# A conditioned attention and state-space block: transposes of u put together ahead of C's, and softplus's guard moved from VectorE to ScalarE

## The chip, the cores and the metric

The kernel runs on one core of one Trainium2 chip. TensorE (PE, with its weight loads listed apart as PEld), VectorE (DVE), ScalarE (ACT), GpSimd (POOL) and SyncE (SP, which only issues transfers here) run side by side, each working down its own list of instructions in order, and wait for each other by semaphores. The metric is the device time of one execution in microseconds (us); lower is better.

## The reference, cut to what matters

The inputs are 8 batch items of 1024 rows by 512 columns. An attention block comes first, then a selective state-space layer. The change touches only the part of that layer between its convolution and its recurrence:

```python
u = silu(conv(x_in))                              # 1024 steps x 1024 channels
x_dbl = u @ x_proj_w.T                            # 64 + 16 + 16 columns
dt_r, B, C = split(x_dbl, [64, 80])
dt = softplus(dt_r @ dt_proj_w.T + dt_proj_b)
def step(h, (dt_t, B_t, C_t, u_t)):               # 16 states per channel
    h = h * exp(dt_t[:, :, None] * A) + (dt_t * u_t)[:, :, None] * B_t[:, None, :]
    y = einsum('bdn,bn->bd', h, C_t)
y = ys + u * D_param                              # then gated by silu(z) and projected
```

## The kernel before

The batch items are worked one after the other (loop `b`). Within an item the attention comes first, then the projections, then the convolution; while an item's recurrence runs, PE and ACT fill their gaps with the previous item's output products and with the next item's front part.

Channels lie on the partitions in 8 tiles of 128 (index n, `ND = NT = 8`), time along the free dimension (1024). The recurrence works on 4 tiles at a time (`DL = 4`), in two groups (`DG = 2`). For each of the 16 states (round r) and each of the 4 tiles, ACT computes the decay exp(dt*A) into PSUM (L892), POOL computes dt*u*B (L693, `inject`), DVE runs the scan (L1172, printed by the order as a SCALAR_TENSOR_TENSOR that writes area_h), PE transposes the state back to rows of time (L1509), and DVE (L1182, `add`) and ACT (L876, `scale_by_c`) each take half of the product with C.

Ahead of the first group's scans stands a stretch that this change rearranges. PE ends the products for x_dbl, and ACT copies them to `xdT` (L870). PE then transposes u, 8 blocks for each of 8 row tiles (L1433, into the PSUM bank pairs 4-5 and 6-7 in turn; tile n may start once DVE has emptied tile n-2), and DVE multiplies each by D into the accumulator (L1147; below "the products with D", signal `s_ai`). Among these PE transposes C (L1439, into banks 2-3) and DVE copies it to `C_nat` (L1151, signal `s_cn`). PE projects dt for one channel tile at a time (`project_dt`, two matrix products of 512 columns through L1251, signal `s_dp`) into the bank pairs 0, 2, 6, 4 for the tiles n mod 4 = 0, 1, 2, 3.

Softplus of a tile takes these steps: DVE adds the bias and takes the minimum with 30 (`clip`, L1139, signal `s_dm`); ACT takes the exponential (L882) and log(1 + x) (L884, signal `s_dl`), both in `soft`; DVE takes the maximum of the result and the unclipped value (L1160, signal `s_dt`) and multiplies u by dt (L1163, signal `s_du`), both in `dt_and_dtu`. Tiles 0 to 3 pass through before the first group's scans and among them, tiles 4 to 7 at the turn from the first group to the second. ACT's list there is: soft(4), one `scale_by_c`, soft(5), one `scale_by_c`, the decay of tile 4, two `scale_by_c`, the decay of tile 5, soft(6), the decay of tile 6, soft(7), the decay of tile 7. The order on every engine is written out by hand; no scheduler moves anything.

Of the kernel before, what the change touches and what calls it, by code (L numbers as in the profile page):

```python
# [9 lines left out]
ACT = mybir.ActivationFunctionType  # L10
P = 128
# [131 lines left out]

    return slice(i, i + n) if isinstance(i, int) else bass.ds(i, n)

PRO = 10


COLS = {}
# [20 lines left out]
def build(nc, x, condT, mask, params, q_w, k_w, v_w, v_b, emb_w, emb_b, out_w, out_b,  # L170
          adaT, ada_b, inT, xpT, dtT, D_row, opT, out):
    ctx = ExitStack()
    with ctx:
        def sb(name, shape):
            return ctx.enter_context(nc.sbuf_tensor(name, shape, F32))
# [89 lines left out]
        def col(name, i, n=1):  # L265
            at = COLS[name][0]
            return par[:, at + i:at + i + n]
# [8 lines left out]
        den = sb("den", [P, TILES])  # L276
        rden = sb("rden", [P, TILES])
        warm = sb("warm", [P, 1])
        z_st = sb("z_st", [P, 512])
        vb_row, ones_row = wdt[96:P, 0:D], wdt[96:P, D:D + P]  # L280

# [13 lines left out]
        def banks(i, n=TB):  # L295
            return ps[:, i:i + n, :].rearrange("p a c -> p (a c)")
# [445 lines left out]
        def _(act):  # L742
# [64 lines left out]
            for b in range(B):  # L807
# [70 lines left out]

                def soft(n):

                    act.wait_ge(*s_dm.at(b, n + 1))
                    nc.scalar.activation(dtmp[:, n % DL, :], dtmp[:, n % DL, :], ACT.Exp).then_inc(s_de.sem, 1)  # L882
                    act.wait_ge(*s_de.at(b, n + 1))
                    nc.scalar.activation(dtmp[:, n % DL, :], dtmp[:, n % DL, :], ACT.Ln, bias=1.0).then_inc(s_dl.sem, 1)  # L884

# [92 lines left out]
        def _(dve):  # L978
# [25 lines left out]
                at += 4  # L1004
            dve.wait_ge(s_ea.sem, 1)
            v.tensor_scalar_mul(negA[:, :], negA[:, :], -1.0).then_inc(s_pro.sem, 1)
            assert at + 1 == PRO
            dve.wait_ge(s_pro.sem, PRO)

            def row_stats(N, src, n):  # L1010
# [35 lines left out]
            for b in range(B):  # L1046
# [87 lines left out]
                                               scalar=col("cw", n * DC + i), in1=cv[:, n % 2, :],  # L1134
                                               op0=ALU.mult, op1=ALU.add).then_inc(s_cv.sem, 1)

                def clip(n):
                    dve.wait_ge(*s_dp.at(b, n + 1))
                    v.tensor_scalar(dtmp[:, n % DL, :], banks(DT_BANK[n % DL]), col("dtb", n), 30.0,  # L1139
                                    ALU.add, ALU.min).then_inc(s_dm.sem, 1)  # L1140


                dve.wait_ge(*s_xpd.at(b, 32))
                dve.wait_ge(*s_x1s.at(b, 16))
                for n in range(NT):
                    dve.wait_ge(*s_ut.at(b, n + 1))
                    v.tensor_tensor(acc[n], ps[:, 4 + 2 * (n % 2):6 + 2 * (n % 2), :], D_bc.rearrange("p (h c) -> p h c", h=DG),  # L1147
                                    ALU.mult).then_inc(s_ai.sem, 1)
                    if n == 1:
                        dve.wait_ge(*s_ct.at(b, 1))  # L1150
                        v.tensor_copy(C_nat[:, :, :], banks(2).rearrange("p (n c) -> p n c", n=NT)[:, :, DTR + NS:XD]  # L1151
                                      ).then_inc(s_cn.sem, 1)
                        clip(0)
                    if n == 3:
                        clip(1)
                dve.wait_ge(*s_ai.at(b, NT))
                dve.wait_ge(*s_cn.at(b, 1))
                def dt_and_dtu(n):
                    dve.wait_ge(*s_dl.at(b, n + 1))
                    v.scalar_tensor_tensor(out=dT[:, n % DL, :], in0=banks(DT_BANK[n % DL]), scalar=col("dtb", n),  # L1160
# [22 lines left out]
                                           op0=ALU.mult, op1=ALU.add).then_inc(s_acc.sem, 1)  # L1183

                dt_and_dtu(0)
                clip(2)
                dt_and_dtu(1)
                clip(3)
                scan(0, 0, 0, 0)
                dt_and_dtu(2)  # L1190
                scan(0, 0, 0, 1)
# [8 lines left out]
                for dl in range(DL):  # L1200
                    scan(0, NS - 1, 1, dl)
                    add(0, NS - 2, 2 * dl)
                clip(4)
                clip(5)
                add(0, NS - 1, 0)
                add(0, NS - 1, 2)
                dt_and_dtu(4)
                add(0, NS - 1, 4)
                dt_and_dtu(5)
                add(0, NS - 1, 6)  # L1210
                clip(6)
                scan(1, 0, 0, 0)
                dt_and_dtu(6)
                clip(7)
                scan(1, 0, 0, 1)
                dt_and_dtu(7)
                scan(1, 0, 0, 2)
# [29 lines left out]
        def _(pe):  # L1247
# [79 lines left out]
            for b in range(B):  # L1327
# [95 lines left out]
                def project_dt(n):  # L1423
                    for th in range(TB):
                        done = mm(ps[:, DT_BANK[n % DL] + th, :], wdt[0:DTR, n * P:(n + 1) * P],
                                  xdT[0:DTR, th * 512:(th + 1) * 512], 0, 0)
                    done.then_inc(s_dp.sem, 1)

                for n in range(NT):
                    if n >= 2:  # L1430
                        pe.wait_ge(*s_ai.at(b, n - 1))
                    for k in range(ND):
                        last = nc.tensor.transpose(ps[:, 4 + 2 * (n % 2) + k // 4, (k % 4) * P:(k % 4 + 1) * P],  # L1433
                                                   U[:, k, n * P:(n + 1) * P], ident[:, :])
                    last.then_inc(s_ut.sem, 1)
                    if n == 1:
                        pe.wait_ge(*s_xde.at(b, 1))
                        for m in range(NT):
                            last = nc.tensor.transpose(ps[:, 2 + m // 4, (m % 4) * P:(m % 4 + 1) * P],  # L1439
                                                       xdT[:, m * P:(m + 1) * P], ident[:, :])  # L1440
                        last.then_inc(s_ct.sem, 1)
                        project_dt(0)
                    if n == 2:
                        pe.wait_ge(*s_cn.at(b, 1))
                        project_dt(1)
                pe.wait_ge(*s_ai.at(b, NT))
                def start_unit(i):
                    if emptied_first(i):
# [41 lines left out]
                            deferred_product(m)  # L1490

                project_dt(2)
                project_dt(3)
                for dg in range(DG):
                    pe.wait_ge(*s_dt.at(b, (dg + 1) * DL))
# [99 lines left out]
```

## Time and profile before

| | |
|---|---|
| median of 3 runs | 6619.38 us (6618.05 to 6626.11) |
| the profiled execution | 6618.08 us, of which its span is 6616.3 us |
| PE busy | 6091.8 us (92%) |
| DVE busy | 5758.6 us (87%) |
| ACT busy | 4575.9 us (69%) |
| POOL busy | 3036.3 us (46%) |
| mean granted TensorE clock | 0.949 of full speed |

Busy shares are means over stages with different limits. In the timeline a row gives the start from the beginning of the span, the time that the merged instructions took, their engine, line, operation, output and inputs; in brackets stands the idle time of the engine just before, with the instruction that ended it. A row with x8 stands for 8 instructions of a kind in a run. On DVE and ACT an instruction's row overlaps the next one's by some tenths of a microsecond, so that the distance between starts is shorter than the duration shown. PE's products in 32-bit floating point appear as two instructions each.

### The profile page before, as it was taken

The page shows a single profiled execution, that of the slowest core. Times are in us where ns is not written, and L with a number is a line of the kernel's source. Part 1 is how long each engine was busy: PE and PEld are TensorE (multiplying, and loading weights), DVE is VectorE, ACT ScalarE, POOL GpSimd, SP SyncE. Part 2 cuts the span into 40 slices and gives each one's busy share as a digit, 9 for nine tenths or more (in the row PEclk, how much of TensorE's full clock was granted, in tenths as well). Part 3 has the DMA queues.
Part 4 walks back from the last instruction along what each step waited for, and adds up shares of the span by engine and source line. Part 5 has one row for each costly group of instructions (what it writes and reads, how often), then busy time and mean ns, then how long its engine had stood idle before and what let it go on. Part 6 is the DMA issues. An engine that isn't in the chain of part 4 may idle for free.

```text
span 6616.3 us, 114602 instructions
## 1 busy us (share of the span) xinstructions
PE 6091.8 (92%) x43104; PEld 3972.8 (60%) x43104; DVE 5758.6 (87%) x7083; ACT 4575.9 (69%) x6560; POOL 3036.3 (46%) x1538
## 2 busy tenths in 40 slices
PE   5998999988999889989899899998899988999877
PEld 2774558645585556845577455774558655685554
DVE  0797999889997999969999799988999789996995
ACT  2775678667786677857778467866778667785653
POOL 0104881068701786019830388105871078601883
PEclk8999999999999999999999999999999999999967
DMA  3535885357834678247863488535784467824764
GB/s 144 172 96 163 204 204 156 115 166 199 237 106 143 166 204 233 85 143 185 216 190 101 146 207 207 160 109 165 195 219 129 136 165 199 240 72 146 178 147 129
DMA packets 326517, 1087.52 MB, mean 164 GB/s; under 512 B 49944, under 2 KB 50072, under 8 KB 286960
## 3 DMA queue, kind: packets, MB, share of 16 engines
q1 hardware_dynamic: 245728, 656.81, 31.0%
q0 software_dynamic: 61840, 390.09, 26.2%
q10 hardware_dynamic: 18432, 33.56, 1.5%
q8 instruction: 344, 5.64, 0.4%
q14 instruction: 173, 1.42, 0.1%
HBM read 570.16 MB, written 241.71 MB: 123 GB/s over the span
## 4 chain that ended last, share of the span: by engine, by line
PE 68%; DVE 21%; issue 5%; POOL 2%; DMA 2%; ACT 2%; SPq 1%; DVEq 0%; ACTq 0%; POOLq 0%
PE ps L1251 39%; DVE area_h L1172 13%; PE ps L1359 13%; PE ps L1509 8%; DVE area_acc L1182 4%; PE ps L1300 3%; POOL area_s L693 2%; PE ps L1302 1%; PE ps L1272 1%; DVE area_dt L1160 1%; DVE area_h L1139 1%; PE ps L1433 1%; PE ps L1456 1%; DVE area_acc L1147 1%; DMA k_stack<-qk_keep 1%
## 5 line engine op out<-in xcount | busy, mean ns | idle before, releaser
L693 POOL TENSOR_TENSOR area_s<-area_u,area_s 128x1024 f32<-128x1024 f32 x1024 | 2495.1, 2450 | 602.2 <-DVE area_u L1163 370.0
L1172 DVE TENSOR_TENSOR_SCAN area_h<-ps,area_s 128x1024 f32<-128x1024 f32 x1024 | 2332.7, 2278 | 18.4 <-POOL area_s L693 17.1
L1509 PEld LDWEIGHTS ps<-ident,area_h 128*128 128x128 f32 x8192 | 984.5, 150 | 776.7 <-DVE area_acc L1182 431.8
L1509 PE MATMUL ps<-ident,area_h 128*128 128x128 f32 x8192 | 1192.0, 293 | 207.2 <-DVE area_acc L1182 142.3
L814 ACT ACTIVATE area_s<-area_s,negmax 128x1024 f32<-128x1024 f32 x1024 | 1179.0, 1151 | 251.4 <-DVE negmax L1068 242.8
L1068 DVE CUSTOM_DVE_ANT_0 area_s<-ps,area_dt 128x1024 f32<-128x1024 f32 x1024 | 1242.8, 1215 | 102.6 <-PE ps L1251 102.1
L892 ACT ACTIVATE ps<-area_dt,negA 128x1024 f32<-128x1024 f32 x1024 | 1146.2, 1119 | 241.3 <-DVE area_h L1172 100.8
L681 POOL TENSOR_TENSOR area_s<-area_s 128x1024 f32<-128x1024 f32 x64 | 161.5, 2524 | 2302.3 <-ACT area_s L867 2302.3
L876 ACT ACTIVATE area_w<-ps,C_nat 128x512 f32<-128x512 f32 x1024 | 703.6, 687 | 688.0 <-PE ps L1509 680.5
L1359 PE MATMUL ps<-ident,area_s 128*128 128x128 f32 x8192 | 1062.0, 272 | 0.4
L1359 PEld LDWEIGHTS ps<-ident,area_s 128*128 128x128 f32 x8192 | 955.1, 141 | 139.2 <-issue 5.2
L1251 PE MATMUL ps<-area_xT,area_w 128*128 128x512 f32 x2048 | 932.3, 594 | 10.7 <-ACT k_stack L791 7.8
L1182 DVE SCALAR_TENSOR_TENSOR area_acc<-ps,C_nat,area_acc 128x512 f32<-128x512 f32 x1024 | 744.0, 727 | 60.8 <-PE ps L1509 60.5
L1087 DVE COPY area_h<-ps 128x512 f32<-128x512 f32 x1024 | 705.4, 689 | 69.1 <-PE ps L1359 63.8
L1251 PE MATMUL ps<-k_stack,q_stack 128*128 128x512 f32 x2048 | 734.7, 440 | 18.6 <-DVE negmax L1068 14.2
L1251 PE MATMUL ps<-area_w,area_xT 128*128 128x512 f32 x1536 | 713.8, 599 | 0.5 <-ACT area_xT L759 0.4
L1251 PEld LDWEIGHTS ps<-area_xT,area_w 128*128 128x128 f32 x2048 | 375.1, 190 | 396.4 <-issue 351.9
L823 ACT ACTIVATE area_h<-ps 128x512 f32<-128x512 f32 x1024 | 589.9, 577 | 10.1 <-PE ps L1359 10.0
L1251 PE MATMUL ps<-area_h,area_u 128*32 128x128 f32 x16384 | 552.5, 276 | 8.6 <-ACT area_h L823 7.0
L1251 PEld LDWEIGHTS ps<-area_h,area_u 128*32 128x32 f32 x16384 | 417.2, 109 | 94.7 <-issue 88.0
L1133 DVE SCALAR_TENSOR_TENSOR area_h<-area_h,par 128x1024 f32<-128x1024 f32 x192 | 290.8, 1523 | 189.9 <-ACT area_h L859 185.3
L1251 PEld LDWEIGHTS ps<-area_w,area_xT 128*128 128x128 f32 x1536 | 274.2, 193 | 248.5 <-issue 248.5
(124 smaller groups left out, 5294.8 us busy)
## 6 DMA issues: line engine op xcount, KB each, us to landing
area_acc<-area_w POOLq DMA_DIRECT2D x256, 1024.0 KB, 7.6
area_s<-b_rows SPq DMA_DIRECT2D x256, 512.0 KB, 4.3
q_stack<-qk_keep SPq DMA_DIRECT2D x512, 128.0 KB, 2.8
k_stack<-qk_keep SPq DMA_DIRECT2D x512, 128.0 KB, 3.1
area_s<-z_keep SPq DMA_DIRECT2D x72, 512.0 KB, 5.0
qk_keep<-q_stack SPq DMA_DIRECT2D x128, 256.0 KB, 4.6
qk_keep<-k_stack SPq DMA_DIRECT2D x128, 256.0 KB, 4.8
y_keep<-area_acc POOLq DMA_DIRECT2D x8, 4096.0 KB, 14.8
```

The lines of the kernel that those rows point to most:

```text
L693: pool.tensor_tensor(dbu[:, dl % 2, :], U[:, k // (NS * DL) * DL + dl, :], bb[:, q, :], ALU.mult).then_inc(s_dbu.sem, 1)
L814: nc.scalar.activation(S[:, t % SR, :], S[:, t % SR, :], ACT.Exp, scale=-1.0, bias=negmax[:, t % TILES:t % TILES + 1], accum_out=den[:, t ...
L823: nc.scalar.activation(PT[:, (t // HALF) % 2, HALF:NT, c * P:(c + 1) * P], ps[:, ring_bank("act", t), :].rearrange("p (m c) -> p m c", m=H ...
L876: nc.scalar.activation(part[slot][:, n // 2, :], ps[:, 5, :], ACT.Identity, scale=C_nat[:, n, r:r + 1]).then_inc(s_ev.sem, 1)
L892: nc.scalar.activation(banks(2 * (dl % 2)), dT[:, dl, :], ACT.Exp, scale=negA[:, a_col:a_col + 1]).then_inc(s_da.sem, 1)
L1068: v.tensor_tensor_reduce(out=S[:, t % SR, :], in0=banks(2 * (t % 2)), in1=mask_add, scale=-1.0, scalar=3.0e38, op0=ALU.add, op1=ALU.min, a ...
L1087: v.tensor_copy(PT[:, (t // HALF) % 2, 0:HALF, c * P:(c + 1) * P], ps[:, ring_bank("dve", t), :].rearrange("p (m c) -> p m c", m=HALF)).th ...
L1172: v.tensor_tensor_scan(out=hs[:, q, dl, :], data0=banks(2 * (dl % 2)), data1=dbu[:, dl % 2, :], initial=0.0, op0=ALU.mult, op1=ALU.add).th ...
L1182: v.scalar_tensor_tensor(out=part, in0=ps[:, 4, :], scalar=c_col, in1=part, op0=ALU.mult, op1=ALU.add).then_inc(s_acc.sem, 1)
L1251: return nc.tensor.matmul(out, lhsT, rhs, start=(k == 0), stop=(k == last))
L1359: last = nc.tensor.transpose(ps[:, ring_bank(who, t), m * P:(m + 1) * P], S[:, t % SR, (c * HALF + m) * P:(c * HALF + m + 1) * P], ident[: ...
L1509: last = nc.tensor.transpose(ps[:, 4 + n % 2, dl * P:(dl + 1) * P], hs[:, r % 2, dl, n * P:(n + 1) * P], ident[:, :])
```

## The change

1. DVE's `clip` is gone, in all eight places. In `soft`, ACT now reads the projection from PSUM and computes relu(16 - bias - x) with scale -1 and a bias column `below_cap`, then exp(16 - that), with scale -1 and a bias column `cap`. This is exp(min(x + bias, 16)). The logarithm is as before. The two columns are made once, ahead of the batch loop, by two small DVE instructions.
2. On PE the transposes of C come after all of u's, into banks 4-5; the projection of dt for tile 1 comes after u's fifth tile instead of the third. The wait for C's copy stands ahead of the projection of tile 3.
3. On DVE the copy of C comes behind the first `dt_and_dtu` instead of behind the second product with D.

```diff
-PRO = 10
+PRO = 12
+CAP = 16.0
...
                 def soft(n):
+                    act.wait_ge(*s_dp.at(b, n + 1))
+                    nc.scalar.activation(dtmp[:, n % DL, :], banks(DT_BANK[n % DL]), ACT.Relu, scale=-1.0,
+                                         bias=below_cap[:, n:n + 1]).then_inc(s_dm.sem, 1)
                     act.wait_ge(*s_dm.at(b, n + 1))
-                    nc.scalar.activation(dtmp[:, n % DL, :], dtmp[:, n % DL, :], ACT.Exp).then_inc(s_de.sem, 1)
+                    nc.scalar.activation(dtmp[:, n % DL, :], dtmp[:, n % DL, :], ACT.Exp, scale=-1.0, bias=cap[:, 0:1]
+                                         ).then_inc(s_de.sem, 1)
...
+            v.tensor_scalar(below_cap[:, :], col("dtb", 0, ND), -1.0, CAP, ALU.mult, ALU.add).then_inc(s_pro.sem, 1)
+            v.memset(cap[:, :], CAP).then_inc(s_pro.sem, 1)
...
-                def clip(n):
-                    dve.wait_ge(*s_dp.at(b, n + 1))
-                    v.tensor_scalar(dtmp[:, n % DL, :], banks(DT_BANK[n % DL]), col("dtb", n), 30.0,
-                                    ALU.add, ALU.min).then_inc(s_dm.sem, 1)
...
-                    if n == 1:
-                        dve.wait_ge(*s_ct.at(b, 1))
-                        v.tensor_copy(C_nat[:, :, :], banks(2).rearrange("p (n c) -> p n c", n=NT)[:, :, DTR + NS:XD]
-                                      ).then_inc(s_cn.sem, 1)
-                        clip(0)
-                    if n == 3:
-                        clip(1)
...
                 dt_and_dtu(0)
-                clip(2)
+                dve.wait_ge(*s_ct.at(b, 1))
+                v.tensor_copy(C_nat[:, :, :], banks(4).rearrange("p (n c) -> p n c", n=NT)[:, :, DTR + NS:XD]
+                              ).then_inc(s_cn.sem, 1)
                 dt_and_dtu(1)
-                clip(3)
+                dve.wait_ge(*s_cn.at(b, 1))
                 scan(0, 0, 0, 0)
...
-                clip(4)
-                clip(5)
                 add(0, NS - 1, 0)
...
-                clip(6)
                 scan(1, 0, 0, 0)
                 dt_and_dtu(6)
-                clip(7)
...
                     if n == 1:
                         pe.wait_ge(*s_xde.at(b, 1))
-                        for m in range(NT):
-                            last = nc.tensor.transpose(ps[:, 2 + m // 4, (m % 4) * P:(m % 4 + 1) * P],
-                                                       xdT[:, m * P:(m + 1) * P], ident[:, :])
-                        last.then_inc(s_ct.sem, 1)
                         project_dt(0)
-                    if n == 2:
-                        pe.wait_ge(*s_cn.at(b, 1))
+                    if n == 4:
                         project_dt(1)
+                pe.wait_ge(*s_ai.at(b, NT - 1))
+                for m in range(NT):
+                    last = nc.tensor.transpose(ps[:, 4 + m // 4, (m % 4) * P:(m % 4 + 1) * P],
+                                               xdT[:, m * P:(m + 1) * P], ident[:, :])
+                last.then_inc(s_ct.sem, 1)
                 pe.wait_ge(*s_ai.at(b, NT))
...
                 project_dt(2)
+                pe.wait_ge(*s_cn.at(b, 1))
                 project_dt(3)
```

On PE, between the products for x_dbl and the first group's state transposes, the kernel before has these rows (`ident,area_u` are u's transposes, `ident,xdT` C's, `xdT,wdt` the projections of dt):

```order
L1433 MATMUL ps<-ident,area_u 128x128 x16
L1439 MATMUL ps<-ident,xdT 128x128 x8
L1251 MATMUL ps<-xdT,wdt 128x512 x2
L1433 MATMUL ps<-ident,area_u 128x128 x8
L1251 MATMUL ps<-xdT,wdt 128x512 x2
L1433 MATMUL ps<-ident,area_u 128x128 x40
L1251 MATMUL ps<-xdT,wdt 128x512 x4
```

In the changed kernel the same place on PE reads:

```order
L1425 MATMUL ps<-ident,area_u 128x128 x16
L1243 MATMUL ps<-xdT,wdt 128x512 x2
L1425 MATMUL ps<-ident,area_u 128x128 x24
L1243 MATMUL ps<-xdT,wdt 128x512 x2
L1425 MATMUL ps<-ident,area_u 128x128 x24
L1435 MATMUL ps<-ident,xdT 128x128 x8
L1243 MATMUL ps<-xdT,wdt 128x512 x4
```

C's transposes moved from third to next to last, and tile 1's projection two of u's tiles later; the sum of the work is the same.

On ACT, at the turn from the first group of channels to the second, the kernel before has (`area_h<-area_h` are softplus's exponential and logarithm, `ps<-area_dt,negA` a decay, `area_w<-ps,C_nat` a product with C):

```order
L882 ACTIVATE area_h<-area_h 128x1024
L884 ACTIVATE area_h<-area_h 128x1024
L876 ACTIVATE area_w<-ps,C_nat 128x512
L882 ACTIVATE area_h<-area_h 128x1024
L884 ACTIVATE area_h<-area_h 128x1024
L876 ACTIVATE area_w<-ps,C_nat 128x512
L892 ACTIVATE ps<-area_dt,negA 128x1024
L876 ACTIVATE area_w<-ps,C_nat 128x512 x2
L892 ACTIVATE ps<-area_dt,negA 128x1024
L882 ACTIVATE area_h<-area_h 128x1024
L884 ACTIVATE area_h<-area_h 128x1024
```

The changed kernel has there:

```order
L884 ACTIVATE area_h<-ps,below_cap 128x1024
L887 ACTIVATE area_h<-area_h,cap 128x1024
L890 ACTIVATE area_h<-area_h 128x1024
L878 ACTIVATE area_w<-ps,C_nat 128x512
L884 ACTIVATE area_h<-ps,below_cap 128x1024
L887 ACTIVATE area_h<-area_h,cap 128x1024
L890 ACTIVATE area_h<-area_h 128x1024
L878 ACTIVATE area_w<-ps,C_nat 128x512
L898 ACTIVATE ps<-area_dt,negA 128x1024
L878 ACTIVATE area_w<-ps,C_nat 128x512 x2
L898 ACTIVATE ps<-area_dt,negA 128x1024
L884 ACTIVATE area_h<-ps,below_cap 128x1024
```

Each softplus has one instruction more, and no table load (ACT_TABLE_LOAD) has been added between them.

## Rows read from the trace of the kernel before

**Rows 1.** The page: busy time, and the chain that ended last by engine.
```profile
PE 6091.8 (92%) x43104; PEld 3972.8 (60%) x43104; DVE 5758.6 (87%) x7083; ACT 4575.9 (69%) x6560; POOL 3036.3 (46%) x1538
PE 68%; DVE 21%; issue 5%; POOL 2%; DMA 2%; ACT 2%; SPq 1%; DVEq 0%; ACTq 0%; POOLq 0%
```

**Rows 2.** Timeline of DVE (start, us, engine, line, ...), second item, first group.
```profile
1366.69 2.36 DVE L1147 TENSOR_TENSOR area_acc<-ps,area_h 128x1024 f32<-128x1024 f32 x2 [8.62 <-PE ps L1433]
1368.96 0.28 DVE L1151 COPY C_nat<-ps 128x128 f32<-128x128 f32 x1
1370.25 1.28 DVE L1139 TENSOR_SCALAR area_h<-ps,par 128x1024 f32<-128x1024 f32 x1 [1.01 <-PE ps L1251]
...
1374.21 1.22 DVE L1147 TENSOR_TENSOR area_acc<-ps,area_h 128x1024 f32<-128x1024 f32 x1 [1.54 <-PE ps L1433]
...
1382.45 1.28 DVE L1160 SCALAR_TENSOR_TENSOR area_dt<-ps,par,area_h 128x1024 f32<-128x1024 f32 x1
...
1384.91 1.28 DVE L1139 TENSOR_SCALAR area_h<-ps,par 128x1024 f32<-128x1024 f32 x1
...
1389.78 2.27 DVE L1172 TENSOR_TENSOR_SCAN area_h<-ps,area_s 128x1024 f32<-128x1024 f32 x1
...
1401.64 4.63 DVE L1172 TENSOR_TENSOR_SCAN area_h<-ps,area_s 128x1024 f32<-128x1024 f32 x2 [0.32 <-POOL area_s L693]
```

**Rows 3.** Timeline of DVE, the same stretch of the fifth item.
```profile
3734.55 2.36 DVE L1147 TENSOR_TENSOR area_acc<-ps,area_h 128x1024 f32<-128x1024 f32 x2 [6.78 <-PE ps L1433]
...
3756.66 2.28 DVE L1172 TENSOR_TENSOR_SCAN area_h<-ps,area_s 128x1024 f32<-128x1024 f32 x1
```

**Rows 4.** Timeline of PE, second item, the stretch of Rows 2.
```profile
1365.52 1.91 PE L1433 MATMUL ps<-ident,area_u 128*128 128x128 f32 x16
1367.27 1.04 PE L1439 MATMUL ps<-ident,xdT 128*128 128x128 f32 x8
1368.23 1.98 PE L1251 MATMUL ps<-xdT,wdt 64*128 64x512 f32 x4
...
1377.81 3.34 PE L1433 MATMUL ps<-ident,area_u 128*128 128x128 f32 x16 [1.23 <-DVE area_acc L1147]
...
1397.91 1.97 PE L1456 MATMUL ps<-ident,area_acc 128*128 128x128 f32 x8 [10.75 <-DVE area_dt L1160]
```

**Rows 5.** Timeline of POOL, the stretch of Rows 2.
```profile
1385.22 2.36 POOL L693 TENSOR_TENSOR area_s<-area_u,area_s 128x1024 f32<-128x1024 f32 x1 [23.14 <-DVE area_u L1163]
```

**Rows 6.** Timeline of SyncE's transfer issues, the stretch of Rows 2.
```profile
1388.72 0.79 SPq L540 DMA_DIRECT2D area_acc<-yg_keep  x2
```

**Rows 7.** Timeline of DVE, second item, turn to the second group.
```profile
1579.52 1.28 DVE L1139 TENSOR_SCALAR area_h<-ps,par 128x1024 f32<-128x1024 f32 x1 [2.54 <-PE ps L1251]
...
1593.01 1.28 DVE L1160 SCALAR_TENSOR_TENSOR area_dt<-ps,par,area_h 128x1024 f32<-128x1024 f32 x1
...
1598.96 1.28 DVE L1160 SCALAR_TENSOR_TENSOR area_dt<-ps,par,area_h 128x1024 f32<-128x1024 f32 x1
```

**Rows 8.** Timeline of ACT, the stretch of Rows 7.
```profile
1578.61 1.06 ACT L882 ACTIVATE area_h<-area_h 128x1024 f32<-128x1024 f32 x1 [0.40 <-ACT z_st L923]
...
1580.66 0.67 ACT L876 ACTIVATE area_w<-ps,C_nat 128x512 f32<-128x512 f32 x1
```

**Rows 9.** Groups of instructions by line: count, busy us, mean ns, idle before.
```profile
L814 ACT ACTIVATE area_s<-area_s,negmax 128x1024 f32<-128x1024 f32 x1024 | 1179.0, 1151 | 251.4 <-DVE negmax L1068 242.8
...
L859 ACT ACTIVATE area_h<-ps,par 128x1024 f32<-128x1024 f32 x64 | 76.7, 1198 | 0.0
...
L882 ACT ACTIVATE area_h<-area_h 128x1024 f32<-128x1024 f32 x64 | 67.6, 1056 | 106.0 <-DVE area_h L1139 102.8 <-ACT z_st L923 3.2
...
L855 ACT ACTIVATE area_h<-ps 128x1024 f32<-128x1024 f32 x64 | 65.2, 1019 | 69.8 <-PE ps L1251 69.3
```

**Rows 10.** PE in stretches: length, busy, granted clock, DMA share, GB/s.
```profile
1378.00:1380.00 2.00, 2.00 (x12) 0.55 0.00 0
...
1588.00:1590.00 2.00, 0.34 (x1) 0.96 1.02 230
1590.00:1592.00 2.00, 2.00 (x3) 0.50 0.96 323
```

More of the change, by code:

```diff
@@ L278, in build @@
         warm = sb("warm", [P, 1])
+        below_cap, cap = sb("below_cap", [P, ND]), sb("cap", [P, 1])
         z_st = sb("z_st", [P, 512])
@@ L1006, in _ @@
             v.tensor_scalar_mul(negA[:, :], negA[:, :], -1.0).then_inc(s_pro.sem, 1)
-            assert at + 1 == PRO
+            v.tensor_scalar(below_cap[:, :], col("dtb", 0, ND), -1.0, CAP, ALU.mult, ALU.add).then_inc(s_pro.sem, 1)
+            v.memset(cap[:, :], CAP).then_inc(s_pro.sem, 1)
+            assert at + 3 == PRO
             dve.wait_ge(s_pro.sem, PRO)
@@ L1148, in _ @@
                                     ALU.mult).then_inc(s_ai.sem, 1)
-                    if n == 1:
-                        dve.wait_ge(*s_ct.at(b, 1))
-                        v.tensor_copy(C_nat[:, :, :], banks(2).rearrange("p (n c) -> p n c", n=NT)[:, :, DTR + NS:XD]
-                                      ).then_inc(s_cn.sem, 1)
-                        clip(0)
-                    if n == 3:
-                        clip(1)
                 dve.wait_ge(*s_ai.at(b, NT))
-                dve.wait_ge(*s_cn.at(b, 1))
                 def dt_and_dtu(n):
```

## The prediction, made before the changed kernel was run

> **What bounds the kernel now.** I read the page first: PE is busy 92% of the span and DVE 87%, and the chain that ended last is 68% PE and 21% DVE [rows 1]. These are means over an item of some 789 us, and the change touches two short places of it, so I went to the timelines there. At both, the reader is to see whose row has no idle time before it and what follows directly.
>
> First place, ahead of the first group's scans, once per item. From the first product with D (1366.69) to the first scan (1389.78) DVE is idle only in short waits for PE (1.01, 1.54 and others); behind 1382.45 it runs without a gap [rows 2]. POOL waits 23.14 us for the first dt*u, then the scans follow it [rows 5]; PE waits 10.75 us for DVE [rows 4]. So DVE's list sets this place, with PE close behind while u is transposed. Whatever comes out of it moves all later work of the item, since PE, ACT and POOL all start from DVE's results.
>
> Second place, the turn to the second group. The second clip stands behind 2.54 us of idle time, ended by PE [rows 7]: PE is still projecting, and DVE's next products with C need PE's transposes, which come behind that projection. Later, from 1582.88, DVE is full to the last scan of the round.
>
> **First place, worked out.** PE's start does not change. The distances between starts at full clock are 0.96 us for 8 transposes (1367.27 to 1368.23) and 1.9 for a projection [rows 4]; a product with D takes 1.22 alone and 1.15 in a run [rows 2]; DVE starts some 1.1 after PE starts a tile. The new order then gives: projection 0 at 1367.27 to 1369.2; u's tile 2 is ready at 1370.3, tile 3 at 1371.3; tile 4 must wait for its banks until 1371.5; projection 1 at 1372.5 to 1374.4; tile 5 ready at 1375.5, multiplied from 1375.6; tile 6 multiplied from 1376.75; tile 7 waits for tile 5's product (1376.8), is ready at 1377.95, and its product ends at 1379.2. That is 12.5 us behind the first product, where it was 15.76 (1382.45 less 1366.69).
>
> Then DVE has the first dt_and_dtu (2.47 to the next start, 1382.45 to 1384.91 before), C's copy (0.28, about 0.2 in a run), the second dt_and_dtu (again 2.47), and no clip (1.2 each). The first scan could start at 12.5 + 2.47 + 0.2 + 2.47 = 17.65. POOL's dt*u*B starts 0.2 behind dt*u (15.3) and takes 2.36, so the scan stands at 17.8: here POOL takes the place of the clips as the last to be ready, but only just. From there to the fourth scan 11.86 us stay as they are (1389.78 to 1401.64): three dt_and_dtu, scans, and the 0.32 wait for POOL.
>
> Before, the first scan is 23.09 behind the first product in this item [rows 2] and 22.11 in the fifth [rows 3]. The eight items show two kinds: two near 23.08, six near 22.0. In the longer kind the last two of u's tiles took PE 3.34 us instead of 1.97, with a granted clock of 0.55 [rows 4, 10]. Gain: 2 x 5.3 + 6 x 4.2 = 35.8 us.
>
> Is ACT in time here? A softplus now takes relu, exp and ln. No row shows a Relu. The nearest from PSUM with 1024 columns are the plain copy (L855) at 1.02 and the one with two columns as operands (L859) at 1.20; Relu has one, so I take 1.11. The exponential takes 1.06 now (L882), and 1.15 where it has a bias column (L814, accumulator included), which I take [rows 9]. A softplus is then 3.38 from start to end (was 2.15) and 3.29 until the next instruction can start (was 2.05, 1578.61 to 1580.66) [rows 8]. Tile 2's logarithm would end at 18.3 and is wanted at 20.0; tile 3's ends at 22.7 and is wanted at 24.6. Both hidden, with 1.7 and 1.9 to spare. C's copy behind the first dt_and_dtu holds back only projection 3, inside the same slack. The flips on PE, behind the fourth dt, need two loads issued at 22.0 [rows 6]; these move up with the products with D, by about 3.2, while the flips move by 5.3: I put the landing 2 us ahead of them, so nothing is late.
>
> **Second place, worked out.** All four clips go, but clips 4 and 5 stood in the wait for PE (2.4 us, nothing back). ACT gets its list longer: it starts soft(4) at 1578.61 as now, and its sum is 3.29 (soft 4) + 0.57 + 3.29 (soft 5) + 0.58 + 1.05 (decay) + 0.58 = 1587.97; the next scale_by_c needs a transpose that needs the one before it, so 1588.75; then 0.58 and a decay 1.05: soft(6) starts at 1590.4 and ends at 1593.8. The dt behind it started at 1593.01 before. Then a chain without slack: dt 1.3, decay 1.1, soft(7) 3.4, and the next dt is at 1599.6, where it was 1598.96 [rows 7]. The clips' time comes back as a wait for ACT, and 0.65 us more. Bounds: with 1.02 and 1.06 for the two instructions this loss is nothing; with 1.20 for both it is 1.2. Over eight items: 5.2 us lost (0 to 10).
>
> The two new DVE instructions ahead of the loop: 0.3 us once, under the 0.5 that two short instructions could take.
>
> **Sum.** 6616.3 - 35.8 + 5.2 + 0.3 = 6586.0 for the span; 1.8 lies around it in the profiled run (6618.08), whose time is 1.3 below the median. Forecast: 6589 us.
>
> **A rule that speaks against the change.** The durations above say that relu costs ACT 1.02 to 1.20 [rows 9] where the clip cost DVE 1.28 [rows 2]. The Trainium skill ("ScalarE: Activation LUTs", Rules for kernel authors) says to use VectorE and not ScalarE for relu, min, add and mul. Its reason, a faster rate in bf16, does not meet these 32-bit rows; what remains of it is that ACT may be the engine with less room, which is the loss of 5.2 at the second place.
>
> **Rivals.**
> - *Every clip comes back.* 64 clips at 1.28 are 82 us; 64 at the 1.2 between starts are 77: 6542. For it: DVE's list is full for most of both places. Against it: the 2.54 wait ahead of clip 5, and the ACT chain. Chance 0.07.
> - *The second place costs more.* PE's clock goes to 0.50 at 1590 [rows 10]. The longer softplus holds back ACT's products with C, on which PE's transposes wait; if that makes the clock fall before the projection of tile 6, this projection takes 1.9 longer and ACT's soft(6) comes some 2 us later: 8 x 2 = 16 more, 6605. For it: PE has only scattered work there. Against it: in this item the fall came after that projection. Chance 0.13. The page "TensorE: Matmul & The Clock Gate" of the Trainium skill (The HAM clock gate) has it that activity releases the throttle and idling brings it back; these rows agree as to direction.
> - *What the first place gives is absorbed.* The rounds that follow are nearly full on PE too; were PE or a transfer to hold them from a fixed start, the gain of 35.8 would be lost, and a loss of 5.2 at the turn partly hidden by the same slack, so about 6620. Against it: PE starts the rounds behind the fourth dt (its wait of 10.75). Chance 0.09.
> - *Slower: the relu from PSUM is slow on ACT.* Each softplus at the second place lies on ACT's chain, so each extra microsecond of relu costs 4 per item there, and beyond 0.95 it also uses up the 1.9 of slack at the first place. The change breaks even where 4x + 0.65 = 4.5, at x = 0.96, a relu of 2.1 us. At 2.4 us (x = 1.3): 8 x (5.8 + 0.7 - 4.5) = 16 slower, 6635. Against it: no ACT row of 1024 columns is above 1.20. Chance 0.06.
>
> The forecast has 0.65. **Range.** Its own is 6578 to 6600: the second place from 0 to 10, and 1 us per item either way in the first, where waits on PE are a few tenths each. For 8 in 10 I reach to the costlier second place: 6572 to 6609. A change under 0.2% (13 us) can't be told from none. Faster: 0.65 + 0.07 + 0.09 of the second rival, and a little of the third: 0.82. Same: 0.11. Slower: 0.07.
>
> **What will show it.** In the changed profile: products with D in one run, ending near 12.5 behind the first; first scan at 17.8, waiting shortly for POOL; relu near 1.11 and exp near 1.15; at the turn, DVE's dt of tiles 6 and 7 behind waits for ACT (about 2 us each), and the third scan of the round 0.65 later behind the first group's last scan than now; DVE's busy time 80 less. It is wrong if the relu is above 1.3, if the turn costs over 2 us per item, or if DVE waits for ACT ahead of tiles 2 and 3.

## The result, and the profile after

| | before | changed |
|---|---|---|
| median | 6619.38 us (6617.9 to 6629.21, 15 runs) | 6608.78 us (6600.3 to 6616.94, 15 runs) |
| span of the profiled execution | 6616.3 us | 6606.9 us |
| ratio, changed to before | | 0.998 (95% interval 0.9972 to 0.9988) |
| DVE busy | 5758.6 us | 5687.7 us |
| ACT busy | 4575.9 us | 4648.5 us |

The change gained 10.6 us where 30.4 were forecast, and the time lies just inside the stated range. The direction was right; the size was a third of what was said.

The changed kernel's page, busy times, for [rows 1]:

```profile
PE 6087.7 (92%) x43104; PEld 3972.8 (60%) x43104; DVE 5687.7 (86%) x7021; ACT 4648.5 (70%) x6624; POOL 3034.7 (46%) x1538
```

The groups of softplus by line in the changed kernel (the numbers behind x are count, busy us and mean ns). The new relu takes 1.10 us and the exponential with its bias column 1.15, where the prediction took 1.11 and 1.15 from [rows 9]; so the prices of the single instructions were not the fault:

```profile
L1157 DVE TENSOR_TENSOR area_u<-area_u,area_dt 128x1024 f32<-128x1024 f32 x64 | 86.5, 1351 | 2.2
L1154 DVE SCALAR_TENSOR_TENSOR area_dt<-ps,par,area_h 128x1024 f32<-128x1024 f32 x64 | 81.5, 1273 | 23.4 <-ACT area_h L890 23.1
...
L887 ACT ACTIVATE area_h<-area_h,cap 128x1024 f32<-128x1024 f32 x64 | 73.5, 1149 | 2.1
L884 ACT ACTIVATE area_h<-ps,below_cap 128x1024 f32<-128x1024 f32 x64 | 70.7, 1104 | 40.0 <-PE ps L1243 36.7 <-ACT z_st L929 3.2
```

Two things stand there that were not there before: DVE waits 23.1 us for softplus's logarithm (L890), and dt*u (L1157), whose 64 instructions took 81.8 us before (L1163), takes 86.5. The second dt*u of each item is 1.0 longer than before (8.0 in all), and the one of tile 5 at the turn is 0.4 shorter (1.23 for 1.65, 3.3 in all). This is part of the reason why DVE's busy time fell by 70.9 us and not by the 80 that the prediction named.

DVE's timeline of the second item at the first place, for [rows 2]:

```profile
1369.64 2.35 DVE L1149 TENSOR_TENSOR area_acc<-ps,area_h 128x1024 f32<-128x1024 f32 x2 [8.63 <-PE ps L1425]
1373.34 3.63 DVE L1149 TENSOR_TENSOR area_acc<-ps,area_h 128x1024 f32<-128x1024 f32 x3 [1.35 <-PE ps L1425]
1378.69 3.63 DVE L1149 TENSOR_TENSOR area_acc<-ps,area_h 128x1024 f32<-128x1024 f32 x3 [1.71 <-PE ps L1425]
1382.35 1.28 DVE L1154 SCALAR_TENSOR_TENSOR area_dt<-ps,par,area_h 128x1024 f32<-128x1024 f32 x1
1383.67 1.23 DVE L1157 TENSOR_TENSOR area_u<-area_u,area_dt 128x1024 f32<-128x1024 f32 x1
1384.82 0.28 DVE L1181 COPY C_nat<-ps 128x128 f32<-128x128 f32 x1
1385.02 1.27 DVE L1154 SCALAR_TENSOR_TENSOR area_dt<-ps,par,area_h 128x1024 f32<-128x1024 f32 x1
1386.32 2.23 DVE L1157 TENSOR_TENSOR area_u<-area_u,area_dt 128x1024 f32<-128x1024 f32 x1
1388.48 2.28 DVE L1166 TENSOR_TENSOR_SCAN area_h<-ps,area_s 128x1024 f32<-128x1024 f32 x1
```

POOL's timeline there, for [rows 5]:

```profile
1385.12 2.35 POOL L695 TENSOR_TENSOR area_s<-area_u,area_s 128x1024 f32<-128x1024 f32 x1 [21.90 <-DVE area_u L1157]
```

The products with D end 12.7 behind the first, where 12.5 was forecast. The second dt*u takes 2.23 us and not 1.23: it starts at 1386.32, while POOL works until 1387.47, and ends 1.08 behind that. The scan comes at 18.84 instead of 17.8. It does not wait for POOL, where the prediction had it wait shortly. (A row of DVE here reaches less than 0.1 us into the next one, not some tenths.)

PE's timeline at the same place, for [rows 4]:

```profile
1381.09 1.09 PE L1435 MATMUL ps<-ident,xdT 128*128 128x128 f32 x8
1382.37 1.98 PE L1243 MATMUL ps<-xdT,wdt 64*128 64x512 f32 x4 [0.19 <-DVE area_acc L1149]
1385.15 3.37 PE L1243 MATMUL ps<-xdT,wdt 64*128 64x512 f32 x4 [0.80 <-DVE C_nat L1181]
```

C's transposes stand in the place that the working gave them. Projection 3 stands behind a wait of 0.80 for C's copy and takes 3.37 in place of 1.98, but DVE has no wait ahead of the dt of tiles 2 and 3.

DVE at the turn to the second group, second item, for [rows 7]:

```profile
1577.94 0.75 DVE L1176 SCALAR_TENSOR_TENSOR area_acc<-ps,C_nat,area_acc 128x512 f32<-128x512 f32 x1 [4.67 <-PE ps L1502]
...
1591.65 1.28 DVE L1154 SCALAR_TENSOR_TENSOR area_dt<-ps,par,area_h 128x1024 f32<-128x1024 f32 x1 [1.94 <-ACT area_h L890]
...
1597.42 1.28 DVE L1154 SCALAR_TENSOR_TENSOR area_dt<-ps,par,area_h 128x1024 f32<-128x1024 f32 x1 [1.03 <-ACT area_h L890]
```

The time of clips 4 and 5 is now a wait of 4.67 for PE. That of clips 6 and 7 is two waits for ACT, of 1.94 and 1.03, where the prediction had about 2 each.

PE at the turn in the first item, where it went worse:

```profile
790.67 0.66 PE L1502 MATMUL ps<-ident,area_h 128*128 128x128 f32 x4 [1.06 <-ACT area_w L878]
791.25 3.39 PE L1243 MATMUL ps<-xdT,wdt 64*128 64x512 f32 x4
794.57 3.93 PE L1502 MATMUL ps<-ident,area_h 128*128 128x128 f32 x16
```

And PE's busy time with its granted clock there, in stretches (length, busy, clock, DMA share, GB/s):

```profile
790.00:792.00 2.00, 1.33 (x6) 0.92 1.04 355
792.00:794.00 2.00, 2.00 (x4) 0.50 1.06 316
```

A projection takes 1.98 at full clock and 3.39 here. The clock fell to half behind a wait of 1.06 for ACT's product with C (L878), which itself stands behind the longer softplus. In the first, fifth and last item the fourth scan of the turn comes 31.6 behind the end of the first group's last scan, in the other five 29.86; before, it was 29.23 to 29.25 in all eight.

The wait alone does not make the difference. PE in the second item, one of the five, has the same wait, and its projection runs at full clock:

```profile
1580.46 0.66 PE L1502 MATMUL ps<-ident,area_h 128*128 128x128 f32 x4 [1.06 <-ACT area_w L878]
1581.05 1.98 PE L1243 MATMUL ps<-xdT,wdt 64*128 64x512 f32 x4
```

All eight items have these two waits of PE, 0.41 and 1.06. By the granted clock of the profile, it fell 8.6 to 8.8 us behind the end of the last scan in the three slow items, and 15.4 to 18.1 behind it in the other five. In the kernel before, PE has one wait of 1.01 in place of these two, and the clock fell 13.9 to 15.2 behind the last scan in all eight. Why three items and not the others is not shown.

Put together from the timeline rows of all eight items, the span of 9.4 less is made up like this:

| part of the span | before | changed | difference |
|---|---|---|---|
| up to the first item's first product with D | 577.5 | 578.5 | +1.1 |
| first product with D to first scan, eight items | 178.2 | 150.8 | -27.4 |
| from there to the end of the first group's last scan | 1475.5 | 1478.5 | +3.0 |
| from there to the fourth scan of the turn | 233.9 | 244.2 | +10.3 |
| from there to the next item's first product with D, or the end | 4151.2 | 4154.9 | +3.7 |

The +3.0 of the third part lies in one distance, that from the first product with C of the group to the second: 28.9 us, summed over the eight items, for 25.7. Without it this part is 1449.6 to 1449.9 in every one of the thirteen profiles of this case. The second product with C waits for PE, and PE works at half clock until then. In the changed kernel the distance is 2.95 in the items where the clock came back 17.6 us behind the first scan, and 4.18 and 4.26 where it came back at 20.1 and 20.2.

### The profile page after: what moved, and what is told of

Same layout as the page of the kernel before. It is cut to its first block, busy times and chain, and to the rows that moved or that the text cites. A ratio compares the mean times of both kernels' runs of the same rounds, so it can differ in the third digit from the quotient of the medians.

```text
span 6606.9 us, 114612 instructions
## 1 busy us (share of the span) xinstructions
PE 6087.7 (92%) x43104; PEld 3972.8 (60%) x43104; DVE 5687.7 (86%) x7021; ACT 4648.5 (70%) x6624; POOL 3034.7 (46%) x1538
## 3 DMA queue, kind: packets, MB, share of 16 engines
q14 instruction: 173, 1.42, 0.1%
## 4 chain that ended last, share of the span: by engine, by line
PE 73%; DVE 17%; issue 3%; ACT 3%; DMA 1%; POOL 1%; SPq 1%; DVEq 0%; ACTq 0%; POOLq 0%
PE ps L1243 42%; PE ps L1351 13%; DVE area_h L1166 11%; PE ps L1502 10%; PE ps L1292 3%; DVE area_acc L1176 3%; POOL area_s L695 1%; PE ps L1294 1%; PE ps L1264 1%; DVE area_dt L1154 1%; PE ps L1448 1%; PE ps L1425 1%; DVE area_u L1157 1%; DMA k_stack<-qk_keep 1%; ACT area_h L887 1%
## 5 line engine op out<-in xcount | busy, mean ns | idle before, releaser
L878 ACT ACTIVATE area_w<-ps,C_nat 128x512 f32<-128x512 f32 x1024 | 703.7, 687 | 692.2 <-PE ps L1502 684.0
L1243 PE MATMUL ps<-area_xT,area_w 128*128 128x512 f32 x2048 | 932.3, 594 | 10.6 <-ACT k_stack L793 7.8
```

The lines of the kernel that those rows point to most:

```text
L878: nc.scalar.activation(part[slot][:, n // 2, :], ps[:, 5, :], ACT.Identity, scale=C_nat[:, n, r:r + 1]).then_inc(s_ev.sem, 1)
L1243: return nc.tensor.matmul(out, lhsT, rhs, start=(k == 0), stop=(k == last))
```

## The experiments

The places given for a run below are read off DVE's timeline in all eight items of its profile, as for the table above. "First scan" is its distance from the item's first product with D; "fourth scan of the turn" its distance from the end of the first group's last scan. The comparisons are with the kernel before on the same chip: medians 6621.69, 6620.27 and 6619.85 in the three groups.

**1. The guard on ACT in the first group only.** `ON_ACT` lists the tiles whose guard is on ACT; the others have their clip on DVE:

```diff
+ON_ACT = (0, 1, 2, 3)
...
+                    if n in ON_ACT:
+                        act.wait_ge(*s_dp.at(b, n + 1))
+                        nc.scalar.activation(dtmp[:, n % DL, :], banks(DT_BANK[n % DL]), ACT.Relu, scale=-1.0,
+                                             bias=below_cap[:, n:n + 1]).then_inc(s_dm.sem, 1)
...
+                    else:
+                        nc.scalar.activation(dtmp[:, n % DL, :], dtmp[:, n % DL, :], ACT.Exp).then_inc(s_de.sem, 1)
...
+                def clip(n):
+                    if n in ON_ACT:
+                        return
```

The calls of `clip` stand again in their old places at the turn.

> The changed kernel with relu on ScalarE for tiles 0 to 3 only; tiles 4 to 7 have their clip on VectorE as before. Theory (the turn to the second group is bound by ScalarE's longer list, the first place is VectorE's): first scan of the first group still 18.85 us behind the first product with D, and the fourth scan of the turn again 29.2 us behind the end of the first group's last scan (29.86 to 31.6 in the changed kernel, 29.23 before); time about 6598. Rival (what the first place gives is absorbed in the rounds whatever the turn does): about 6609, as the changed kernel.

Measured: 6594.04 us (ratio 0.996, 0.9946 to 0.9973). First scan 18.85 in all items, fourth scan of the turn 29.23 or 29.24 in all. So the loss at the turn comes from the guard there, and without it the kernel is 27.6 us faster than before in the median, which is the 27.4 of the first place. The rival, that the rounds absorb it, falls.

**2. The guard on ACT in the second group only**, everything else as before the change (`ON_ACT = (4, 5, 6, 7)`).

> The kernel before with relu on ScalarE for tiles 4 to 7 only; the first place is as before. Theory (ScalarE's list at the turn): fourth scan of the turn 29.9 behind the last scan of the first group, 31.6 in items where TensorE's clock falls before the projection of tile 6; time 6624 to 6634, slower than before. Rival (the clips removed on VectorE are worth something at the turn too): below 6619.

Measured: 6631.74 us (1.0015, 1.0006 to 1.0024), 10 us slower. Fourth scan of the turn 29.87 in five items and 31.6 in three. DVE has four instructions less there, and the kernel is slower. This and run 1 together give -17.6, while the whole change gave -10.6. The 7 us between are not accounted for by the parts; the interval of run 1 alone is some 9 us wide to either side, so they may be noise.

**3. The order alone**, all eight clips on DVE:

```diff
+                    if n == 1:
+                        clip(0)
+                    if n == 4:
+                        clip(1)
...
                 dt_and_dtu(0)
+                clip(2)
                 dve.wait_ge(*s_ct.at(b, 1))
```

> The order of the changed kernel on TensorE and VectorE, with all eight clips still on VectorE (clip of tile 1 behind the fifth product with D, where its projection now comes). Theory: first scan 20.5 behind the first product with D, against 22.0 to 23.1 before and 18.85 changed; turn as before; time about 6605. Rival (the order gives nothing by itself, all comes from the clips): first scan at 22, time 6619.

Measured: 6614.94 us (0.9988, 0.9979 to 0.9997). First scan 20.56 in five items, 21.2 to 22.1 in three: there the projection of tile 3 runs in part or wholly at half clock, and clip 3 waits 0.52 to 1.42 for it. The order by itself is worth 10.1 us at the first scans (168.1 against 178.2) and 7 in the median. The time is 10 us above the expectation of 6605; the three slow items are 4 of these, the rest is not placed.

**4. The guard alone**, for all tiles, with C's transposes and copy where they were.

> The kernel before with relu on ScalarE for all eight tiles, the transposes and the copy of C where they were. Theory: first scan 19.6 behind the first product with D (0.8 later than in the changed kernel), turn as in the changed kernel; time about 6615. Rival (the order matters more than the guard): 6620 or above.

Measured: 6618.89 us (0.9996, 0.9987 to 1.0005). First scan 19.71, turn 29.87 in five items and 31.6 in three. The guard gives 20.5 at the first scans and loses 10.3 at the turn. Of the 10.2 between them nothing is left that is clear of noise in the median (2.8 faster); in the profile the two other parts of the item are 4.5 and 6.5 longer. The time is 4 above the expectation of 6615, the places are where they were expected.

**5. Is it POOL that holds the second dt*u?**

```diff
-                    pool.wait_ge(*s_du.at(b, k // (NS * DL) * DL + dl + 1))
+                    pool.wait_ge(*s_du.at(b, 2 if k == 0 else k // (NS * DL) * DL + dl + 1))
```

> The changed kernel, but GpSimd's first dt*u*B of each item waits for the second dt*u instead of the first. Theory (VectorE's second dt*u, 2.23 us instead of 1.23, stands still while GpSimd works on its first dt*u*B): the second dt*u takes 1.23 again, GpSimd ends at about 20.3 behind the first product with D, the first scan comes at 20.4 instead of 18.85; time about 6621. Rival (the second dt*u is long for another reason, as ScalarE's reads of PSUM or a transfer): it still takes 2.2.

Measured: 6617.53 us (0.9997, 0.9988 to 1.0007). DVE in the second item:

```profile
1386.63 1.28 DVE L1154 SCALAR_TENSOR_TENSOR area_dt<-ps,par,area_h 128x1024 f32<-128x1024 f32 x1
1387.94 1.23 DVE L1157 TENSOR_TENSOR area_u<-area_u,area_dt 128x1024 f32<-128x1024 f32 x1
1391.93 2.29 DVE L1166 TENSOR_TENSOR_SCAN area_h<-ps,area_s 128x1024 f32<-128x1024 f32 x1 [2.76 <-POOL area_s L695]
```

POOL there:

```profile
1389.39 4.65 POOL L695 TENSOR_TENSOR area_s<-area_u,area_s 128x1024 f32<-128x1024 f32 x2 [24.55 <-DVE area_u L1157]
```

With POOL idle the second dt*u takes 1.23 in all eight items. The scan is later (20.68), since POOL now starts last; the run shows the cause and is no cure. The scan came 0.3 later than expected, 0.2 of it because POOL starts that much behind the end of the second dt*u.

**6. Does a wait of PE let the clock fall at the turn?** One product more, in that wait:

```diff
                         for n in range(NT):
+                            if r == NS - 1 and n == 3:
+                                pe.wait_ge(*s_ge.at(b, NU - 1))
+                                for f in range(1):
+                                    nc.tensor.matmul(ps[:, 6, :], ident[:, :], hs[:, r % 2, 0, 0:512], start=True, stop=True)
```

> The changed kernel with one more product of 512 columns on TensorE (result unused, overwritten by the projection of tile 6) in its wait for ScalarE at the turn. Theory (waits of TensorE for ScalarE let its clock fall before the projection of tile 6, in 3 of 8 items, 1.8 us each): the fourth scan of the turn 29.9 behind the last scan in all or nearly all items; time about 6604. Rival (the clock falls for something else, the phase of an item): 31.6 in about 3 of 8 items as before, time 6609.

Measured: 6602.13 us (0.9974, 0.9964 to 0.9984), 6.7 below the changed kernel's median. PE in the first item:

```profile
788.65 0.66 PE L1506 MATMUL ps<-ident,area_h 128*128 128x128 f32 x4 [0.41 <-DVE area_acc L1176]
789.14 1.02 PE L1502 MATMUL ps<-area_h,ident 128*128 128x512 f32 x2
790.43 0.66 PE L1506 MATMUL ps<-ident,area_h 128*128 128x128 f32 x4 [0.26 <-ACT area_w L878]
791.01 1.98 PE L1243 MATMUL ps<-xdT,wdt 64*128 64x512 f32 x4
```

The wait of 1.06 is 0.26, and the projection takes 1.98. The fourth scan of the turn is at 29.86 to 29.94 in all eight items. Useless work made the kernel faster. Five profiles with the full guard at the turn and no such product had 3, 3, 3, 2 and 1 slow items of 8 (the last with POOL's late start, run 5); this has none. One profile without a slow item could be chance where 12 of 40 are slow, but the times point the same way: the nine executions here took 6598.7 to 6604.6 us, the 25 of the changed kernel in its two measurements 6600.3 to 6616.9, with medians of 6608.8 and 6611.3.

**7. Clips 4 and 5 back on DVE**, where DVE waits for PE anyway (`ON_ACT = (0, 1, 2, 3, 6, 7)`).

> The changed kernel with the clips of tiles 4 and 5 back on VectorE, where they stand in its wait for TensorE; tiles 6 and 7 keep relu on ScalarE. Theory (ScalarE's chain sets the turn, clips 4 and 5 cost VectorE nothing): fourth scan of the turn 28.35 behind the last scan, 0.9 earlier than before the change and 1.5 than with it; time about 6587. Rival (TensorE or the clock sets the turn as soon as ScalarE is faster): 29.2, time as with the guard moved in the first group alone, 6594.

Measured: 6588.05 us (0.9953, 0.9939 to 0.9966). Fourth scan of the turn at 28.33 or 28.34 in all items: both clips cost DVE nothing, and ACT's chain is shorter by two relus.

**8. The same, and softplus of tile 7 ahead of the decay of tile 6.**

```diff
                 soft(6)
+                soft(7)
                 decay_tile(1, 0, 2)
-                soft(7)
                 decay_tile(1, 0, 3)
```

> As the kernel with the clips of tiles 4 and 5 on VectorE, and ScalarE does softplus of tile 7 ahead of the decay of tile 6, which takes VectorE's dt of tile 6 out of its chain. Theory: fourth scan of the turn 27.2 behind the last scan; time about 6578. Rival (the decay of tile 6 comes late and holds the third scan): 28.4 or more, time 6587.

Measured: 6580.85 us (0.9943, 0.993 to 0.9957). Fourth scan of the turn at 27.2 in all items, 1.1 earlier than in run 7.

**9. The version with the lowest median: dt of tile 0 in DVE's wait for PE.** Run 8, and

```diff
                                     ALU.mult).then_inc(s_ai.sem, 1)
+                    if n == 4:
+                        dt_of(0)
...
                 def dt_and_dtu(n):
+                    if n:
+                        dt_of(n)
```

where `dt_of` is the first half of `dt_and_dtu`.

> The kernel with clips 4 and 5 on VectorE and softplus of tile 7 early, and the dt of tile 0 put between the fifth and the sixth product with D, where VectorE waits 1.71 us for TensorE. Theory (one list on VectorE, with the second dt*u standing still until GpSimd's first dt*u*B is done): products with D still end 12.7 behind the first, first scan at 17.6 instead of 18.85, time about 6571. Rival (TensorE's transposes are late by what VectorE does in between, or GpSimd's end sets the scan at the old place): first scan at 18.5 or later, 6580.

Measured: 6575.46 us (0.9933, 0.9919 to 0.9946). DVE in the second item:

```profile
1365.97 3.63 DVE L1166 TENSOR_TENSOR area_acc<-ps,area_h 128x1024 f32<-128x1024 f32 x3 [1.35 <-PE ps L1449]
1369.53 1.27 DVE L1152 SCALAR_TENSOR_TENSOR area_dt<-ps,par,area_h 128x1024 f32<-128x1024 f32 x1
1371.32 3.63 DVE L1166 TENSOR_TENSOR area_acc<-ps,area_h 128x1024 f32<-128x1024 f32 x3 [0.52 <-PE ps L1449]
...
1377.64 2.23 DVE L1175 TENSOR_TENSOR area_u<-area_u,area_dt 128x1024 f32<-128x1024 f32 x1
1379.80 2.28 DVE L1184 TENSOR_TENSOR_SCAN area_h<-ps,area_s 128x1024 f32<-128x1024 f32 x1
```

The wait of 1.71 is 0.52, and the first scan comes at 17.53 in all items. The second dt*u still takes 2.23. The first scans give 10.6 us over run 8, the median gives 5.4, and the intervals of the two ratios overlap, so the places show this gain more clearly than the time does. Half of it is lost behind the first scan: the second product with C follows the first 3.2 to 4.0 later here, where the profiles of runs 7 and 8 have 2.8 to 3.4. The clock came back 18.2 to 19.8 behind the first scan here, in run 8 at 17.1 to 17.8.

**10 and 11. Both kernels once more.**

> The changed kernel once more, for a second profile. Theory (the first place and the turn are the same in each execution, the granted clock is not): first scan at 18.85 in all items, fourth scan of the turn at 29.86, or 31.6 in a few items that need not be the first, fifth and last; time 6605 to 6612. Rival (the clock falls at the same items each time): again the first, the fifth and the last.

Measured: 6611.26 us (0.9985, 0.9975 to 0.9994). First scan 18.85 in all items; slow turns (31.6) in the first and fourth item, not in the fifth and last. PE has the same two waits of 0.41 and 1.06 in all eight items again.

> The kernel before once more, for a second profile. Theory: fourth scan of the turn at 29.23 in all items; from there to the next item's first product with D 553 to 556; a sum over the items within 3 of the first profile's. Rival (the rest of the item is shorter before than after, so the change costs something there too): a sum below 4152 again, where the changed kernel has over 4154.

Measured: one time, 6628.58 us; span 6626.8. Fourth scan of the turn 29.23 or 29.24. The part from there to the next item sums to 4161.6, against 4151.2 in the first profile: 10 us apart in one and the same kernel. So the +3.7 of the changed kernel in that part says nothing of the change. The expectation that the two would agree within 3 was wrong.

## Why the prediction came out as it did

- **First place, products with D: right but for 0.2.** They end at 12.7 for 12.5; the order on PE did what the schedule said.
- **First place, the step that failed:** "the second dt_and_dtu (again 2.47)". It took 3.46. Before, clip 2 stood between the two dt*u, and POOL's first dt*u*B was all but over when the second began: it began at 1387.42 and POOL ended at 1387.58 [rows 5]. With the clip gone the second dt*u starts 1.15 before POOL ends, and stands still. Run 5 shows it by taking POOL away. The price came from rows in which POOL was nearly done, and was used where POOL was in the middle of its work. The first scan is 1.05 us later than forecast, 8.4 in all: 27.4 for 35.8. Of the 1.05, 0.99 is the standing still, 0.2 the later products with D, and 0.15 came back, because DVE no longer waits for POOL at the scan. The trace of before had a row that shows the standing still at the turn, and it was not read:

```profile
1587.30 1.65 DVE L1163 TENSOR_TENSOR area_u<-area_u,area_dt 128x1024 f32<-128x1024 f32 x1
```

  POOL worked from 1585.50 to 1587.87 there; this dt*u ends at 1588.95, again 1.08 behind. It stands so in all sixteen items of the two profiles of the kernel before. The Trainium skill has the rule ("SBUF — State Buffer", SBUF: two separate sides): VectorE with two SBUF inputs and a GpSimd operation that reads SBUF exclude each other for a whole instruction, the later one blocks. These rows agree that the later one is held: it ends 1.08 behind GpSimd's end, where 1.23 would be its whole duration.

- **Second place, the chain: right in size where it ran at full clock.** It lost 0.63 per item for 0.65, in five of eight items. **The second step that failed** is the term of 5.2 for the whole turn, which lost 10.3: the rival "the second place costs more" came true in three items, at 1.7 to 1.8 each (2 was its price, for all eight). Runs 2, 4, 5 and 10 show, as the changed kernel's own profile does, that one and the same turn has it in some items and in others not, 12 of 40 in all. The prediction made it a case of its own with a chance of 0.13, all items or none, where it belonged into the sum with a share. Its sign of being wrong, a turn that costs over 2 us per item, came true in these three items and not in the mean (1.3).
- **Behind the first scan:** +3.0, where the prediction had nothing. It is the distance from the first to the second product with C (28.9 for 25.7). Across the profiles this sum runs from 23.5 (run 8) to 30.2 (run 4), and it goes with the clock: 2.84 in an item where the clock came back by 17.4 us behind the first scan, and about half a microsecond more for each microsecond that it came later. All but one of the 104 items of the thirteen profiles lie on this line within 0.1. Why the clock comes back sooner in some items is not settled, so it is not shown that the change has a part in it.
- **The other rivals.** "Every clip comes back" is refuted by run 2, "absorbed" by run 1, and "slow relu" by the 1.10 us that it took. The Trainium skill has the rule to use VectorE and not ScalarE for relu, min and add ("ScalarE: Activation LUTs", Rules for kernel authors). By duration it does not hold here: the relu took 1.10 us on ScalarE, the clip, an add and a minimum, 1.28 on VectorE. At the turn, where ACT had no room, following it would have been right (run 1).
- **Sum.** -35.8 + 8.4 (first place) + 5.2 + 5.1 (turn) + 3.0 (clock behind the first scan) + 3.7 + 1.1 (the rest and the start) = -9.3 of span, -9.4 before rounding. The last two are noise as far as is known: the two profiles of the kernel before differ by 10.3 and 1.2 in these parts. The term of 0.3 for the two new instructions was small as forecast; they took 0.16 and 0.06 us. That the range still held the time owes something to its edge, which had been drawn to reach the costlier turn.

## What to carry to other kernels

Moving work off the busiest engine is worth only what that engine's list is worth at that place: the same edit gave 20.5 us where VectorE had no gaps and cost 10.3 where it had waited for TensorE and the receiving engine was the chain. Decide it tile by tile: with clips 4 and 5 left on VectorE and softplus of tile 7 moved up the kernel is at 6581, where moving everything is at 6609. And when an instruction is taken out between two others, ask what ran on the neighbouring engine while it ran: what comes forward may meet it. A duration holds only for what the neighbour did in the rows that it was read from.

## What the runs showed of the hardware that was not expected

- A VectorE product of two SBUF operands (dt*u, 1.23 us) that starts while GpSimd works on dt*u*B ends 1.08 to 1.09 us behind GpSimd's end. It takes 1.65 when it starts 1.8 us into GpSimd's instruction, 2.23 when it starts 1.2 into it (all items of every kernel with the new order and no clip between, run 5 apart) and 2.42 when it starts 1.0 into it (run 4). VectorE's operations with one operand in PSUM (dt, 1.28; the scan, 2.28) ran beside GpSimd unchanged.
- With TensorE waits of 0.41 and 1.06 us at the turn, the granted clock fell 8.6 to 8.9 us behind the last scan in 12 of 40 items, and 15.4 to 18.6 behind it in the other 28, where the waits are the same; an early fall cost 1.7 to 1.8 us. With one wait of 1.01 in their place it fell at 13.9 to 15.2 in all 16 items of the kernel before. One unused product of 1.02 us in the longer wait went with no early fall in eight items.
- Work that waits for TensorE at half clock is moved by the moment at which the clock comes back: the second product with C of a group came 2.84 to 4.26 us behind the first, in step with it.
- Two executions of one kernel differ by 10 us in a part that holds no change; single profiles are good for places, not for the sum.
